# Rows of f2 by DMA through DRAM instead of transposes and a spreading matmul, in a two-layer graph attention kernel

## The chip, the core and the metric

The kernel runs on one core of a Trainium2 chip. The metric is the device time of one execution in microseconds: median 1540.99 of 3 runs (1539.92 to 1544.33). All times below are microseconds unless marked ns.

## The reference

For each of 16 graphs (512 nodes, 256 features), one shared adjacency:

```
h   = relu(layernorm(x))
for each of 4 heads:  Wh = h @ W[head]                       # 512 x 256
    f1 = Wh @ a1[head];  f2 = Wh @ a2[head]                  # one number per node
    e[n, m] = leaky_relu(f1[n] + f2[m], 0.01);  masked by adj # 512 x 512
    out[head] = elu(softmax(e) @ Wh)
then the same attention once more ("BACK") on the 4 joined heads (W_out, a_out)
y   = relu(out @ w1 + b1) @ w2 + b2 + out;  x = x + layernorm(y) * gamma + beta
h   = relu(layernorm(x))
x   = x + deg * (h @ Wi.T + b) + adj @ (h @ Wj.T)
```

What matters here is f2: it is made as a column (one number per node, nodes on the partitions) and is needed as a row in every partition, to be added to the mask and reduced to each row's maximum.

## The kernel before

All weights, the mask and the transposed adjacency stay in SBUF. The loop goes over the 16 batches (graphs), software-pipelined: every engine has an order table, `(step, info, late)`, written out by hand at the head of the file. In round t an engine goes through its table once and does each step for batch t - late (19 rounds in all, the first and last partly empty). Each engine executes in order; steps of different engines are tied by semaphores. TensorE computes the products in float32r with a high and a low part of each operand, thus three matmuls per product.

A batch has ten units: heads 0 and 1, BACK, heads 2 and 3, each in two halves of 256 rows (two groups of 128). A unit goes: `rowmax` (VectorE, L604 to L611: f2 row plus mask, written to `arg`, maximum to `gmax`), `rowmath`, `args` (ScalarE, two leaky relus and two exponentials in place), `turn_p` (TensorE, eight transposes to psR), `probs` (ScalarE the high part, VectorE the low part), `attend` (24 matmuls), `elu_in`, `elu_low` (GpSimd), `elu_exp`, `elu_out`. `arg` has ARGS = 3 buffers; a row max of unit u waits until `turn_p` of unit u - 3 is done.

The other steps of a round: `turn_in` and `m1` (eight of 12 matmuls, one per head and half; VectorE's part of it reads psA into `whx_lo` and `fcol`), `turn2` and `mix2` (four each: eight transposes of `hcat`, 24 matmuls), `turn_out`, `ffn1`, `ffn2`, `norm_ff`, `gamma` and `x_beta` (GpSimd), `x2`, `norm_gc`, `turn_gc`, `conv_in`, `conv`. Four double banks of PSUM: psA0, psA1 in turn for all wide products, psR for `turn_p`, psT (banks T0 and T1) for all else, among it the transposes of `turn2`.

f2 of heads before: `f2rows` (L590 to L602 on VectorE, L762 to L769 on TensorE, L406 to L409 on ScalarE) takes the columns of two heads from `fcol`, splits them into a high and a low part, turns them by four transposes into 4 rows of bank T0 and copies these to `f2row`. Then `spread` (L771 to L781) puts the sum of the two rows of a head into all 128 partitions of a bank of psT by one matmul with a 0/1 matrix `pick`; the bank stays taken until the head's second row max has been made. Three f2rows (heads 0 and 1, BACK, heads 2 and 3) and five spreads a round. SP's queue holds only a load, a store and a `load_back` of 512 KB for each batch; the load_back waits for the store's landing.

Of the kernel before, what the change touches and what calls it, by code (L numbers as in the profile page):

```python
# [921 lines left out]
```

## Time and profile before

| | |
|---|---|
| median of the runs | 1540.99 |
| the profiled execution's own time | 1542.53 |
| its span, first to last instruction | 1540.7 |
| TensorE busy | 1428.9 (93%) |
| VectorE, ScalarE, GpSimd busy | 1136.4, 1066.9, 236.3 |
| mean granted TensorE clock | 0.974 of full speed |
| moved by DMA | 33.04 MB |

Busy time of an engine is the time in which at least one of its instructions runs; matmuls are pipelined, so that several overlap, and the busy time of a group of matmuls can be more than what the group costs. An entry of the timeline gives start and length. Idle time stands in brackets with what ended it. PE is TensorE, DVE VectorE, ACT ScalarE, POOL GpSimd, SPq the DMA queue of SyncE.

### The profile page before, as it was taken

The numbers are of one execution on the slowest core, as the hardware profiler recorded it, in microseconds if no ns is written. First come the engines' busy times: TensorE is split into PE (matmuls) and PEld (weight loads), VectorE is DVE, ScalarE is ACT, GpSimd is POOL, SyncE is SP. The second block draws the span as 40 slices with busy tenths as digits, with TensorE's granted clock in tenths as the row PEclk, the third lists the DMA queues.
The fourth block names the chain that finished last, engine by engine and source line by source line (L and its number), as shares of the span: only waits on it lengthen the run. The fifth ranks groups of instructions, "written<-read, shape, count | busy, mean of one in ns | idle before, by whom it ended". The sixth has DMA issues, their size and how long they took to land.

```text
span 1540.7 us, 28639 instructions
## 1 busy us (share of the span) xinstructions
PE 1428.9 (93%) x10792; PEld 1333.2 (87%) x10792; DVE 1136.4 (74%) x2836; ACT 1066.9 (69%) x1700; POOL 236.3 (15%) x254
## 2 busy tenths in 40 slices
PE   1589999999999999999999999999999999999883
PEld 1479899999999999999999999999999999999762
DVE  6666778687778868687887868787886878787533
...
DMA packets 30056, 33.04 MB, mean 21 GB/s; under 512 B 1248, under 2 KB 28896, under 8 KB 29792
## 3 DMA queue, kind: packets, MB, share of 16 engines
q1 hardware_dynamic: 29920, 31.20, 6.3%
...
q14 instruction: 48, 0.39, 0.1%
...
## 4 chain that ended last, share of the span: by engine, by line
PE 81%; ACT 8%; DVE 7%; issue 3%; DMA 0%; POOL 0%; POOLq 0%; DVEq 0%; ACTq 0%
PE psA L736 52%; PE psR L789 8%; PE psT L890 4%; PE psT L814 4%; PE psA L848 4%; PE psA L859 4%; ACT ff L389 2%; ACT arg L420 1%; DVE hx_lo L577 1%; PE psT L780 1%; ACT prob_hi L426 1%; ACT hx_hi L441 1%; PE psT L768 1%; DVE arg L609 1%; PE psT L747 1%
## 5 line engine op out<-in xcount | busy, mean ns | idle before, releaser
L736 PE MATMUL psA<-whx_hi,prob_hi 128*128 128x258 f32 x1024 | 303.4, 296 | 14.2 <-DVE fcol L588 13.6
L736 PE MATMUL psA<-whx_hi,prob_lo 128*128 128x258 f32 x1024 | 291.0, 284 | 0.0
L736 PE MATMUL psA<-whx_lo,prob_hi 128*128 128x256 f32 x1024 | 289.9, 283 | 0.0
L577 DVE TENSOR_TENSOR prob_lo<-psR,prob_hi 128x1024 fp32r<-128x1024 f32 x160 | 195.2, 1220 | 55.5 <-ACT prob_hi L426 55.3
L356 POOL TENSOR_SCALAR elu_ex<-elu_in 128x512 f32<-128x512 f32 x160 | 103.4, 646 | 854.1 <-ACT elu_in L432 702.1
L609 DVE CUSTOM_DVE_ANT_0 arg<-psT,mask 128x512 f32<-128x512 f32 x320 | 208.0, 687 | 27.4 <-PE psT L780 24.4
L416 ACT ACTIVATE arg<-arg,fcol 128x512 f32<-128x512 f32 x320 | 212.5, 714 | 18.0 <-DVE gmax L609 18.0
L420 ACT ACTIVATE arg<-arg,nmax 128x512 f32<-128x512 f32 x320 | 212.0, 712 | 10.5 <-DVE nmax L620 10.5
L736 PEld LDWEIGHTS psA<-whx_hi,prob_hi 128*128 128x128 f32 x1024 | 195.8, 191 | 23.0 <-issue 17.8
L736 PEld LDWEIGHTS psA<-whx_hi,prob_lo 128*128 128x128 f32 x1024 | 194.9, 190 | 4.9 <-issue 3.6
L736 PEld LDWEIGHTS psA<-whx_lo,prob_hi 128*128 128x128 f32 x1024 | 195.6, 191 | 0.0
L426 ACT ACTIVATE prob_hi<-psR 128x1024 fp32r<-128x1024 f32 x160 | 163.1, 1019 | 45.2 <-PE psR L789 44.5
L789 PE MATMUL psR<-ident,arg 128*128 128x128 f32 x1280 | 168.2, 275 | 17.3 <-ACT arg L420 9.0
L789 PEld LDWEIGHTS psR<-ident,arg 128*128 128x128 f32 x1280 | 144.9, 142 | 25.3 <-ACT arg L420 13.9
L736 PE MATMUL psA<-wh_hi,hT_hi 128*128 128x258 f32 x512 | 153.5, 300 | 6.4 <-DVE fcol L588 4.0
L736 PE MATMUL psA<-wo_hi,hx_hi 128*128 128x258 f32 x512 | 147.9, 289 | 0.0
L736 PE MATMUL psA<-wh_lo,hT_hi 128*128 128x258 f32 x512 | 146.0, 285 | 0.0
L736 PE MATMUL psA<-wh_hi,hT_lo 128*128 128x258 f32 x512 | 145.7, 285 | 0.0
L736 PE MATMUL psA<-wo_hi,hx_lo 128*128 128x258 f32 x512 | 145.0, 283 | 0.0
L736 PE MATMUL psA<-wo_lo,hx_hi 128*128 128x258 f32 x512 | 144.9, 283 | 0.0
L404 ACT ACTIVATE whx_hi<-psA 128x512 fp32r<-128x512 f32 x128 | 76.4, 597 | 88.3 <-PE psA L736 88.3
L642 DVE SCALAR_TENSOR_TENSOR hcat<-elu_ex,elu_in 128x512 f32<-128x512 f32 x128 | 111.3, 869 | 27.2 <-ACT elu_ex L436 27.2
...
## 6 DMA issues: line engine op xcount, KB each, us to landing
xin<-in_x SPq DMA_DIRECT2D x16, 512.0 KB, 4.0
xb<-in_x SPq DMA_DIRECT2D x16, 512.0 KB, 3.9
out_x<-xb SPq DMA_DIRECT2D x16, 512.0 KB, 2.9
...
hcat<-in_L_gnn_W_heads SPq DMA_DIRECT2D x2, 512.0 KB, 8.1
...
xb<-in_L_gnn_W SPq DMA_DIRECT2D x1, 512.0 KB, 6.6
```

What stands on the lines that cost most here:

```text
L356: pool.tensor_scalar(elu_ex[:, c.buf, :, :], elu_in[:, c.buf, :, :], 0.0, -3.0e38, ALU.min, ALU.max).then_inc(elu_low, 1)
L404: act.activation(whx[:, 2 * p:2 * p + 2, h, 0:F], psA[c.pair][:, :, 0:F], ACT.Copy).then_inc(m1_hi, 1)
L416: act.activation(a[:, n, :], a[:, n, :], ACT.Prelu, bias=f1[:, n:n + 1], alpha=SLOPE).then_inc(arg_lin, 1)
L420: i = act.activation(a[:, n, :], a[:, n, :], ACT.Exp, bias=nmax[:, c.abuf, n:n + 1])
L426: act.activation(prob[0][:, c.buf, :, :].rearrange("p j i -> p (j i)"), psR[:, :, :].rearrange("p a n -> p (a n)"), ACT.Copy).then_inc(pro ...
L577: return dve.tensor_tensor(out=dst, in0=src, in1=hi.bitcast(fp32), op=ALU.subtract)
L609: dve.tensor_tensor_reduce(out=arg[:, c.abuf, n, :], in0=psT[:, bank_of(c.h), :], in1=mask[:, 2 * c.u + n, :], scale=1.0, scalar=-3.0e38, ...
L642: dve.scalar_tensor_tensor(out=dst, in0=elu_ex[:, c.buf, :, :], scalar=-1.0, in1=elu_in[:, c.buf, :, :], op0=ALU.add, op1=ALU.max).then_in ...
L736: i = pe.matmul(o, a, b_, start=(k == 0), stop=(k == n - 1))
L789: i = pe.transpose(p[:, j, n, :], arg[:, c.abuf, n, j * P:(j + 1) * P], ident[:, :])
L814: i = pe.transpose(psT[:, k // 4, (k % 4) * P:(k % 4 + 1) * P], hcat[:, n, k // KC, (k % KC) * P:(k % KC + 1) * P], ident[:, :])
L848: i = pe.matmul(psA[c.pair][:, o, :], w1_sb[:, k, o * P:(o + 1) * P], outT[:, k, :], start=(k == 0), stop=(k == KC - 1))
```

## The change

`f2rows` and `spread` go from all three tables. In their place SP has a step `f2` for each head: it waits for the column in `fcol` (or `fcol2`), issues a DMA of the 512 numbers to one of four rows of a DRAM scratch, waits for its landing, and issues a DMA that reads this row into all 128 partitions of one of F2S = 3 buffers `f2bc` in SBUF. The row max waits for that landing and reads `f2bc` in place of psT. ARGS goes from 3 to 2, and a row max waits for `turn_p` of unit u - 2. `c1`, `f2row`, their memsets and semaphores go; a spill buffer of the setup moves from `arg` to `f2bc`. All five order tables are written anew. The diff shows the tables of SP and TensorE before and after, and those of the other engines after.

```diff
-    ("load", 0, 3), ("store", 0, 6), ("load_back", 0, 5),
+    ("store", 0, 4), ("load_back", 0, 3), ("load", 0, 0), ("f2", 0, 1), ("f2", 1, 1), ("f2", -1, 2), ("f2", 2, 1),
+    ("f2", 3, 1),
...
 PE_STEPS = [
-    ("conv", 0, 3), ("turn_p", 7, 1), ("attend", 6, 1), ("turn_out", 0, 2), ("turn_p", 8, 1), ("attend", 7, 1),
-    ("ffn1", 0, 2), ("attend", 8, 1), ("turn_p", 9, 1), ("ffn2", 0, 2), ("turn2", 0, 1), ("attend", 9, 1), ("turn2", 1, 1),
-    ("mix2", 0, 1), ("turn_in", 0, 0), ("mix2", 1, 1), ("turn2", 2, 1), ("m1", (0, 0), 0), ("m1", (0, 1), 0),
-    ("turn2", 3, 1), ("m1", (1, 0), 0), ("m1", (1, 1), 0), ("m1", (2, 0), 0), ("f2rows", 0, 0), ("m1", (2, 1), 0),
-    ("spread", (0, 0), 0), ("mix2", 2, 1), ("mix2", 3, 1), ("spread", (0, 1), 0), ("turn_p", 0, 0), ("m1", (3, 0), 0),
-    ("m1", (3, 1), 0), ("turn_p", 1, 0), ("turn_gc", 0, 2), ("attend", 0, 0), ("f2rows", 2, 1), ("turn_p", 2, 0),
-    ("spread", (2, 0), 1), ("attend", 1, 0), ("conv_in", 0, 2), ("f2rows", 1, 0), ("turn_p", 3, 0), ("attend", 2, 0),
-    ("turn_p", 4, 1), ("spread", (1, 0), 0), ("conv_in", 1, 2), ("attend", 3, 0), ("turn_p", 5, 1), ("spread", (1, 1), 0),
-    ("attend", 4, 1), ("turn_p", 6, 0), ("attend", 5, 1),
+    ("mix2", 0, 2), ("turn2", 2, 2), ("mix2", 1, 2), ("m1", (2, 0), 1), ("turn2", 3, 2), ("turn_p", 0, 1), ("m1", (2, 1), 1),
+    ("mix2", 2, 2), ("mix2", 3, 2), ("turn_p", 1, 1), ("attend", 0, 1), ("turn_p", 2, 1), ("turn_gc", 0, 3),
+    ("attend", 1, 1), ("m1", (3, 0), 1), ("turn_p", 3, 1), ("m1", (3, 1), 1), ("conv_in", 0, 3), ("attend", 2, 1),
+    ("turn_p", 4, 2), ("conv_in", 1, 3), ("attend", 3, 1), ("turn_p", 5, 2), ("attend", 4, 2), ("turn_p", 6, 1),
+    ("conv", 0, 3), ("attend", 5, 2), ("turn_p", 7, 1), ("attend", 6, 1), ("turn_p", 8, 1), ("attend", 7, 1),
+    ("turn_out", 0, 2), ("attend", 8, 1), ("turn_p", 9, 1), ("ffn1", 0, 2), ("turn_in", 0, 0), ("attend", 9, 1),
+    ("m1", (0, 0), 0), ("turn2", 0, 1), ("ffn2", 0, 2), ("m1", (0, 1), 0), ("m1", (1, 0), 0), ("turn2", 1, 1),
+    ("m1", (1, 1), 0),
...
 ACT_STEPS = [
...
+    ("m1", (0, 0), 1), ("turn2", 0, 2), ("m1", (0, 1), 1), ("elu_exp", 9, 2), ("m1", (1, 0), 1), ("turn2", 1, 2),
+    ("m1", (1, 1), 1), ("norm_ff_out", 0, 3), ("turn2", 2, 2), ("args", 0, 1), ("mix2", 0, 2), ("m1", (2, 0), 1),
+    ("turn2", 3, 2), ("args", 1, 1), ("probs", 0, 1), ("m1", (2, 1), 1), ("args", 2, 1), ("mix2", 1, 2), ("probs", 1, 1),
+    ("norm_gc_out", 0, 3), ("probs", 2, 1), ("elu_in", 0, 1), ("turn_gc", 0, 3), ("args", 3, 1), ("elu_in", 1, 1),
+    ("m1", (3, 0), 1), ("elu_exp", 0, 1), ("probs", 3, 1), ("elu_exp", 1, 1), ("m1", (3, 1), 1), ("args", 4, 2),
+    ("conv_in", 0, 3), ("args", 5, 2), ("elu_in", 2, 1), ("probs", 4, 2), ("conv_in", 1, 3), ("elu_exp", 2, 1),
+    ("args", 6, 1), ("probs", 5, 2), ("elu_in", 3, 1), ("elu_exp", 3, 1), ("elu_in", 4, 2), ("probs", 6, 1),
+    ("elu_exp", 4, 2), ("args", 7, 1), ("args", 8, 1), ("probs", 7, 1), ("elu_in", 5, 2), ("norm_in_out", 0, 0),
+    ("elu_exp", 5, 2), ("probs", 8, 1), ("elu_in", 6, 1), ("args", 9, 1), ("turn_out", 0, 2), ("elu_in", 7, 1),
+    ("elu_exp", 6, 1), ("elu_exp", 7, 1), ("probs", 9, 1), ("elu_in", 8, 1), ("elu_exp", 8, 1), ("turn_in", 0, 0),
+    ("ffn1", 0, 2), ("elu_in", 9, 1),
 ]
 DVE_STEPS = [
...
+    ("ffn2", 0, 3), ("norm_ff", 0, 3), ("m1", (0, 1), 1), ("m1", (1, 0), 1), ("turn2", 1, 2), ("m1", (1, 1), 1),
+    ("norm_ff_out", 0, 3), ("elu_out", 9, 2), ("rowmax", 0, 1), ("rowmath", 0, 1), ("rowmax", 1, 1), ("turn2", 2, 2),
+    ("x2", 0, 3), ("mix2", 0, 2), ("rowmath", 1, 1), ("m1", (2, 0), 1), ("turn2", 3, 2), ("rowmax", 2, 1), ("rowmath", 2, 1),
+    ("norm_gc", 0, 3), ("probs", 0, 1), ("m1", (2, 1), 1), ("norm_gc_out", 0, 3), ("mix2", 1, 2), ("probs", 1, 1),
+    ("rowmax", 3, 1), ("elu_in", 0, 1), ("rowmath", 3, 1), ("probs", 2, 1), ("turn_gc", 0, 3), ("elu_in", 1, 1),
+    ("rowmax", 4, 2), ("rowmath", 4, 2), ("m1", (3, 0), 1), ("rowmax", 5, 2), ("rowmath", 5, 2), ("elu_out", 0, 1),
+    ("m1", (3, 1), 1), ("probs", 3, 1), ("conv_in", 0, 3), ("elu_in", 2, 1), ("rowmax", 6, 1), ("rowmath", 6, 1),
+    ("elu_out", 1, 1), ("probs", 4, 2), ("conv_in", 1, 3), ("elu_out", 2, 1), ("elu_in", 3, 1), ("rowmax", 7, 1),
+    ("probs", 5, 2), ("elu_in", 4, 2), ("rowmath", 7, 1), ("norm_in", 0, 0), ("rowmax", 8, 1), ("norm_in_out", 0, 0),
+    ("rowmath", 8, 1), ("probs", 6, 1), ("elu_out", 3, 1), ("elu_out", 4, 2), ("conv", 0, 3), ("elu_in", 5, 2),
+    ("probs", 7, 1), ("elu_in", 6, 1), ("rowmax", 9, 1), ("rowmath", 9, 1), ("elu_out", 5, 2), ("probs", 8, 1),
+    ("elu_in", 7, 1), ("elu_out", 6, 1), ("elu_in", 8, 1), ("probs", 9, 1), ("elu_out", 7, 1), ("turn_in", 0, 0),
+    ("elu_out", 8, 1), ("elu_in", 9, 1), ("m1", (0, 0), 0), ("turn2", 0, 1),
 ]
 POOL_STEPS = [
...
+    ("gamma", 0, 3), ("norm_gc", 0, 3), ("elu_low", 0, 1), ("elu_low", 1, 1), ("elu_low", 2, 1), ("elu_low", 3, 1),
+    ("elu_low", 4, 2), ("norm_in", 0, 0), ("elu_low", 5, 2), ("elu_low", 6, 1), ("x_beta", 0, 2), ("elu_low", 7, 1),
+    ("elu_low", 8, 1), ("elu_low", 9, 1), ("norm_ff", 0, 2),
...
-    ARGS = 3
+    ARGS = 2
+    F2S = 3
...
-        c1 = [sb(f"c1_{q}", [P, NC, 2, 2]) for q in range(3)]
...
-        f2row = sb("f2row", [P, N], f32r)
+        f2bc = sb("f2bc", [P, F2S, N])
+        f2_rows = nc.dram_tensor("f2_rows", (4, N), fp32, kind="Internal").ap()
...
+            def f2(c):
+
+                h = c.info
+                head = unit_number[c.b, h, 0] // 2
+                if h == BACK:
+                    sp.wait_ge(m2_read, 2 * (c.b + 1))
+                    column = fcol2[:, :, 0, 1]
+                else:
+                    sp.wait_ge(m1_read, 2 * H * c.b + 2 * h + 2)
+                    column = fcol[:, :, h, 1]
+                wait(sp, max_made, 4 * (head - F2S + 1))
+                sp.dma_start(f2_rows[head % 4].rearrange("(n q) -> q n", q=P), column, allow_slow_non_contiguous=True).then_inc(f2_out, 16)
+                sp.wait_ge(f2_out, 16 * (head + 1))
+                sp.dma_start(f2bc[:, head % F2S, :], f2_rows[head % 4].partition_broadcast(P)).then_inc(f2_spread[head % F2S], 16)
+
...
-            def f2rows(c):
-                q = c.info
-                act.wait_ge(c1_turned[q], c.b + 1)
-                act.activation(f2row[0:4, :], psT[0:4, 0, :], ACT.Copy).then_inc(f2row_made[q], 1)
-
...
             def rowmax(c):
 
-                dve.wait_ge(f2_spread, c.unit // 2 + 1)
+                head = c.unit // 2
+                dve.wait_ge(f2_spread[head % F2S], 16 * (head // F2S + 1))
                 wait(dve, p_turned, c.unit - ARGS + 1)
                 for n in range(2):
-                    dve.tensor_tensor_reduce(out=arg[:, c.abuf, n, :], in0=psT[:, bank_of(c.h), :], in1=mask[:, 2 * c.u + n, :],
+                    dve.tensor_tensor_reduce(out=arg[:, c.abuf, n, :], in0=f2bc[:, head % F2S, :], in1=mask[:, 2 * c.u + n, :],
                                              scale=1.0, scalar=-3.0e38, op0=ALU.add, op1=ALU.max,
                                              accum_out=gmax[:, c.abuf, n:n + 1]).then_inc(max_made, 1)
 
...
-            def f2rows(c):
-                q = c.info
-                pe.wait_ge(c1_made[q], 2 * (c.b + 1))
-                take("T0")
-                for n in range(NC):
-                    i = pe.transpose(psT[0:4, 0, n * P:(n + 1) * P], c1[q][:, n, :, :].rearrange("p a h -> p (a h)"), ident[:, :])
-                i.then_inc(c1_turned[q], 1)
-                lend(("T0",), (f2row_made[q], c.b + 1))
-
-            def spread_(c):
-
-                q, hh = c.info
-                h0, _ = heads_of(q)
-                h = h0 if h0 == BACK else h0 + hh
-                pe.wait_ge(f2row_made[q], c.b + 1)
-                bank = f"T{bank_of(h)}"
-                take(bank)
-                pe.matmul(psT[:, bank_of(h), :], pick[:, hh, :], f2row[:, :], start=True, stop=True).then_inc(f2_spread, 1)
-                lend((bank,), (max_made, 2 * unit_number[c.b, h, 1] + 2))
-
```

## Rows read from the trace of the kernel before

**Rows 1.** The page: busy us, share of the span and instructions of each engine.

```profile
PE 1428.9 (93%) x10792; PEld 1333.2 (87%) x10792; DVE 1136.4 (74%) x2836; ACT 1066.9 (69%) x1700; POOL 236.3 (15%) x254
```

**Rows 2.** The windows: busy us (and instructions) of each engine in one steady round.

```profile
700.00:788.04 88.04, 87.28 (x674) 81.83 (x672) 68.54 (x171) 65.75 (x107) 14.64 (x15) 1.00 0.06 19
```

**Rows 3.** The waits of PE between 200 and 1400 us: total, times, longest.

```profile
PE psR L789 <- ACT arg L420: 3.9, 14, 0.3
```

**Rows 4.** Groups by line, all of the span: busy us, mean ns; idle before, releaser.

```profile
L780 PE MATMUL psT<-f2row,pick 128*128 128x512 f32 x80 | 35.6, 447 | 0.8 <-ACT f2row L409 0.8
...
L768 PE MATMUL psT<-ident,c 128*4 128x128 f32 x192 | 29.1, 275 | 3.5 <-DVE h2T_lo L577 2.5 <-DVE gmax L609 0.8 <-DVE c L602 0.2
```

**Rows 5.** The timeline of PE at a spreading matmul and at four transposes: start, length.

```profile
752.89 0.39 PE L780 MATMUL psT<-f2row,pick 128*128 128x512 f32 x1
753.12 0.28 PE L736 MATMUL psA<-wo_hi,hx_hi 128*128 128x258 f32 x1
...
776.07 0.60 PE L768 MATMUL psT<-ident,c 128*4 128x128 f32 x4
776.50 0.27 PE L789 MATMUL psR<-ident,arg 128*128 128x128 f32 x1
```

**Rows 6.** Groups by line of VectorE and ScalarE on the new chain.

```profile
L416 ACT ACTIVATE arg<-arg,fcol 128x512 f32<-128x512 f32 x320 | 212.5, 714 | 18.0 <-DVE gmax L609 18.0
...
L609 DVE CUSTOM_DVE_ANT_0 arg<-psT,mask 128x512 f32<-128x512 f32 x320 | 208.0, 687 | 27.4 <-PE psT L780 24.4 <-PE psR L789 2.9
...
L577 DVE TENSOR_TENSOR hx_lo<-psT,hx_hi 128x1024 fp32r<-128x1024 f32 x64 | 78.4, 1225 | 16.8 <-ACT hx_hi L441 15.9
...
L558 DVE BATCH_NORM_STATS2 st<-wk 128x6 f32<-128x256 f32 x64 | 22.4, 413 | 0.0
...
L660 DVE TENSOR_TENSOR wk<-psA,wk 128x1024 f32<-128x1024 f32 x16 | 19.3, 1209 | 12.5 <-PE psA L859 12.5
...
L563 DVE BATCH_NORM_AGGREGATE mv_ff<-st 128x2 f32<-128x6 f32 x64 | 6.1, 157 | 1.7
...
L515 DVE CUSTOM_DVE_ANT_0 arg<-hcat,ff 128x256 f32<-128x256 f32 x16 | 5.8, 419 | 0.1
```

**Rows 7.** The timeline of VectorE and GpSimd at 727 us, and gamma's group by line.

```profile
727.59 2.19 DVE L642 SCALAR_TENSOR_TENSOR hcat<-elu_ex,elu_in 128x512 f32<-128x512 f32 x1 [0.68 <-ACT elu_ex L436]
...
726.87 2.36 POOL L360 TENSOR_TENSOR xb<-xb,beta_bc 128x1024 f32<-128x1024 f32 x1
...
L365 POOL TENSOR_TENSOR wk<-wk,gamma_bc 128x1024 f32<-128x1024 f32 x16 | 38.2, 2390 | 71.3 <-ACT wk L389 71.3
```

**Rows 8.** The timeline of SP's queue: the store and the load_back that waits for it.

```profile
447.19 0.38 SPq L324 DMA_DIRECT2D out_x<-xb  x1
450.18 0.37 SPq L320 DMA_DIRECT2D xb<-in_x  x1
```

**Rows 9.** DMA: the queue's share; issues with KB and us to landing; b1c's issue.

```profile
q1 hardware_dynamic: 29920, 31.20, 6.3%
...
xb<-in_x SPq DMA_DIRECT2D x16, 512.0 KB, 3.9
...
gamma_bc<-in_L_gnn_ln_gamma SPq DMA_DIRECT2D x1, 128.0 KB, 6.3
...
b1c<-in_L_gnn_b SPq DMA_DIRECT2D x1, 1.0 KB, 7.7
...
11.55 0.88 SPq L308 DMA_DIRECT2D b1c<-in_L_gnn_b  x1
```

**Rows 10.** The timeline of PE: first and last matmul of an attend, the transposes behind.

```profile
700.03 0.28 PE L736 MATMUL psA<-w2x_hi,prob_lo 128*128 128x258 f32 x1
...
702.77 1.04 PE L789 MATMUL psR<-ident,arg 128*128 128x128 f32 x8
703.56 0.36 PE L736 MATMUL psA<-w2x_hi,prob_hi 128*128 128x258 f32 x1
```

**Rows 11.** The timeline of PE in the drain, with its wait in brackets.

```profile
1465.44 1.01 PE L768 MATMUL psT<-ident,c 128*4 128x128 f32 x4 [2.47 <-DVE h2T_lo L577]
```

More of the change, by code:

```diff
@@ L37 @@
-    ("m1", (2, 1), 1), ("rowmax", 2, 1), ("norm_gc_out", 0, 3), ("mix2", 1, 2), ("probs", 0, 1), ("rowmax", 3, 1),
-    ("m1", (3, 0), 1), ("f2rows", 2, 2), ("rowmath", 2, 1), ("probs", 1, 1), ("turn_gc", 0, 3), ("elu_in", 0, 1),
-    ("m1", (3, 1), 1), ("rowmath", 3, 1), ("f2rows", 1, 1), ("rowmax", 4, 2), ("rowmath", 4, 2), ("rowmax", 5, 2),
-    ("probs", 2, 1), ("elu_in", 1, 1), ("rowmath", 5, 2), ("conv_in", 0, 3), ("probs", 3, 1), ("elu_out", 0, 1),
-    ("elu_in", 2, 1), ("rowmax", 6, 1), ("rowmath", 6, 1), ("rowmax", 7, 1), ("probs", 4, 2), ("conv_in", 1, 3),
@@ L42 @@
-    ("elu_out", 1, 1), ("rowmath", 7, 1), ("elu_in", 3, 1), ("rowmax", 8, 1), ("probs", 5, 2), ("elu_out", 2, 1),
-    ("elu_in", 4, 2), ("rowmax", 9, 1), ("rowmath", 8, 1), ("rowmath", 9, 1), ("probs", 6, 1), ("elu_out", 3, 1),
-    ("elu_in", 5, 2), ("norm_in", 0, 0), ("elu_out", 4, 2), ("elu_out", 5, 2), ("conv", 0, 3), ("probs", 7, 1),
-    ("elu_in", 6, 1), ("probs", 8, 1), ("elu_in", 7, 1), ("elu_out", 6, 1), ("elu_in", 8, 1), ("elu_out", 7, 1),
-    ("norm_in_out", 0, 0), ("elu_out", 8, 1), ("probs", 9, 1), ("ffn2", 0, 2), ("turn2", 0, 1), ("norm_ff", 0, 2),
@@ L47 @@
-    ("elu_in", 9, 1), ("turn2", 1, 1), ("norm_ff_out", 0, 2), ("elu_out", 9, 1), ("turn_in", 0, 0), ("mix2", 0, 1),
-    ("turn2", 2, 1), ("m1", (0, 0), 0),
+    ("ffn2", 0, 3), ("norm_ff", 0, 3), ("m1", (0, 1), 1), ("m1", (1, 0), 1), ("turn2", 1, 2), ("m1", (1, 1), 1),
+    ("norm_ff_out", 0, 3), ("elu_out", 9, 2), ("rowmax", 0, 1), ("rowmath", 0, 1), ("rowmax", 1, 1), ("turn2", 2, 2),
+    ("x2", 0, 3), ("mix2", 0, 2), ("rowmath", 1, 1), ("m1", (2, 0), 1), ("turn2", 3, 2), ("rowmax", 2, 1), ("rowmath", 2, 1),
@@ L49 @@
 ]
 POOL_STEPS = [
-    ("norm_gc", 0, 3), ("elu_low", 0, 1), ("elu_low", 1, 1), ("elu_low", 2, 1), ("elu_low", 3, 1), ("elu_low", 4, 2),
-    ("elu_low", 5, 2), ("elu_low", 6, 1), ("elu_low", 7, 1), ("norm_in", 0, 0), ("elu_low", 8, 1), ("x_beta", 0, 2),
-    ("norm_ff", 0, 2), ("elu_low", 9, 1), ("gamma", 0, 2),
+    ("gamma", 0, 3), ("norm_gc", 0, 3), ("elu_low", 0, 1), ("elu_low", 1, 1), ("elu_low", 2, 1), ("elu_low", 3, 1),
+    ("elu_low", 4, 2), ("norm_in", 0, 0), ("elu_low", 5, 2), ("elu_low", 6, 1), ("x_beta", 0, 2), ("elu_low", 7, 1),
@@ L176, in gnn_kernel @@
         m1_read = sem("m1_read")
-        c1_made = [sem(f"c1_made{q}") for q in range(3)]
-        c1_turned = [sem(f"c1_turned{q}") for q in range(3)]
-        f2row_made = [sem(f"f2row_made{q}") for q in range(3)]
-        f2_spread = sem("f2_spread")
+        f2_out = sem("f2_out")
+        f2_spread = [sem(f"f2_spread{i}") for i in range(F2S)]
         m2_turned = sem("m2_turned")
@@ L324, in store @@
                 sp.dma_start(out_v[c.b], xb[:, :, :]).then_inc(stored, 16)
-            run_all(SP_STEPS, {"load": load, "load_back": load_back, "store": store})
+            run_all(SP_STEPS, {"load": load, "f2": f2, "load_back": load_back, "store": store})
             sp.wait_ge(stored, 16 * B)
@@ L340, in _ @@
                 pool.wait_ge(s_const, 2 + z)
-            pool.memset(f2row[:, :].bitcast(fp32), 0.0)
-            for q in range(3):
-                i = pool.memset(c1[q][:, :, :, :], 0.0)
-            i.then_inc(s_cleared, 1)
             def norm(k):
@@ L689, in _ @@
             run_all(DVE_STEPS, {"norm_in": norm("in", xin, x_loaded, 16), "norm_in_out": norm_out("in"), "turn_in": turn_in, "m1": m1,
-                                "f2rows": f2rows, "rowmax": rowmax, "rowmath": rowmath, "probs": probs, "elu_in": elu_in_,
+                                "rowmax": rowmax, "rowmath": rowmath, "probs": probs, "elu_in": elu_in_,
                                 "elu_out": elu_out_, "turn2": turn2, "mix2": mix2, "ffn2": ffn2,
@@ L893, in conv @@
                 lend(T, (res_ready, c.b + 1))
-            run_all(PE_STEPS, {"turn_in": turn_in, "m1": m1, "f2rows": f2rows, "spread": spread_, "turn_p": turn_p,
+            run_all(PE_STEPS, {"turn_in": turn_in, "m1": m1, "turn_p": turn_p,
                                "attend": attend, "turn2": turn2, "mix2": mix2, "turn_out": turn_out, "ffn1": ffn1, "ffn2": ffn2,
```

33 lines of the change are left out of this document (2 added, 31 removed), and 3 rows, old and new, of the table ACT_STEPS.

## The prediction

> **What bounds the kernel now.** I read the page's busy shares first: TensorE is busy for 93% of the span, VectorE 74% [rows 1]. Then the windows. One steady batch (a round of the order tables) takes 88.04 us from one batch's spreading matmul to the next one's; in it TensorE is busy 87.28, VectorE 68.54, ScalarE 65.75, GpSimd 14.64 us, at granted clock 1.00, the upper level of 2.4 GHz [rows 2]. That leaves 0.76 us a round in which TensorE isn't busy. Third, its waits between 200 and 1400 us: the longest group is 3.9 us in 14 times, none over 0.3 [rows 3]. So in the steady part the time is the sum of TensorE's instructions; a microsecond taken off it is won only if nothing else becomes late, and VectorE, the next engine, has 20 us of room per round on average, but it works strictly in its written order.
>
> **The change part by part.**
>
> *Removed from TensorE.* Per round three groups of four transposes (48 groups, x192) and five spreading matmuls (x80); as busy time 29.1 + 35.6 = 64.7 us in all, 3.6 to 4.0 per round [rows 4]. Busy times of pipelined matmuls overlap, so I price by distances of starts. A spread starts at 752.89 and the next matmul at 753.12: 0.23 us, five of them 1.15. A group of four transposes holds 0.43 (776.07 to 776.50): three of them 1.3 [rows 5]. A matmul behind transposes is longer by 0.08 (0.36 at 703.56 against 0.28 at 700.03 [rows 10]), and four such changes go: 0.3. Sum 2.8 us a round, 16 rounds: **45 us off**. Bounds: 2.5 (40 us) and the busy time, 58 us (3.6 a round).
>
> *Removed elsewhere.* ScalarE loses 48 copies of the f2 rows and VectorE 96 small operations on the columns: neither engine is the sum, so this counts nothing by itself; it is cover for the rest. The memsets at the start lie beside loads: nothing.
>
> *Row max from SBUF instead of PSUM.* The same operation with both operands in SBUF stands in the setup: 128x256 in 420 ns, against 687 ns for 128x512 from PSUM [rows 6]. The slope between them is (687 - 420) / 256 = 1.04 ns an element, that of VectorE's other rows from either memory: no gain, no loss, taken as 0 (bounds -0.1 and +0.1 us an instruction). But now it reads two SBUF operands, and the trace has a row of what that can mean: an elu_out, whose operands are both in SBUF, took 2.19 us from 727.59 (a row max of that size 0.69), and ended 0.55 us after GpSimd's 2.36 us addition that had begun at 726.87 [rows 7]. It stood still until GpSimd was through, and the new row max can do the same. The Trainium skill, page "SBUF — State Buffer", says why: a VectorE instruction with two SBUF inputs and a GpSimd instruction that reads SBUF need the same shared port, held for a whole instruction, and the later one waits. By that rule the old row max (one operand in PSUM) was exempt and the new one is not, and a row max that meets gamma loses all of it, which gives rival 2's 1541; the row on elu_out agrees with the rule, while the row alone leaves open how often they meet.
>
> *The new chain of f2.* Per head SP issues a DMA of 512 single elements from the column to a DRAM row, waits until it has landed, and issues the broadcast of that row to 128 partitions. The trace has neither. Nearest rows: SP begins the store at 447.19, and the load_back that waits for its landing begins at 450.18, 2.99 us on [rows 8]; a load lands in 3.9 [rows 9]. Of that the 512 KB themselves are 1.6 us: 31.2 MB took 6.3% of 1540.7 us, 0.32 MB/us [rows 9]. So a nearly empty store is 3.0 - 1.6 = 1.4, plus the longer issue of single elements (0.88 in the queue against 0.38, b1c against the store [rows 8, 9]) 0.5, plus 0.3 that I grant 512 elements: 2.2. The broadcast is 256 KB: 3.9 - 1.6 + 0.8 = 3.1. Sum **5.3 us**. High ends from the crowded start: b1c's 256 single elements landed in 7.7, gamma's broadcast in 6.3 [rows 9], together 14; these queued behind megabytes, so I stay at the quiet rows. Low end 4.5. The Trainium skill, page "DMA: Bandwidth & Descriptors" (Specifications), says that under 512 B a DMA reads, modifies and writes; no row prices that for a write to DRAM, and it would push the first term up only.
>
> *Where that chain lies.* Four of the five heads have much time; head 0 does not. In the new order TensorE has, between the end of ffn2 and turn2(3), 96 matmuls at 0.119 (23 starts from 700.03 to 702.77) = 11.4 and two groups of eight transposes at 0.87 (0.79 and the change): **13.2 us** [rows 10]. What must be done in that time stands in VectorE's order, one after the other: ffn2's addition 1.21, norm_ff's four statistics 4 x 0.35 = 1.4 and aggregations (0.16 each, in series with the addition behind) 0.7, m1(0,1)'s reading 0.76 (half of turn2's subtraction and a copy), then the f2 chain 5.3, then the row max of units 0 and 1 (four at 208.0 / 320 = 0.65, and rowmath between) 2.9, then turn2(2)'s subtraction 1.2, which frees the psT banks for turn2(3): **13.5 us** [rows 6]. So TensorE is 0.3 us late there in each round, and every microsecond more in the DMA chain is one more. turn2(2), x2, mix2(0) and m1(2,0) of VectorE stand behind the waiting row max, and turn_p(0), mix2(2) and m1(2,1) of TensorE wait for them. I add the port: gamma on GpSimd (2.39 us [rows 7]) waits for norm_ff's output on ScalarE, which follows VectorE's norm_ff_out just before elu_out(9) and rowmax(0): by the durations it becomes ready within 0.3 us of the f2 row. Either it gets between the four row maxima and VectorE loses up to 2.4 us, or it waits for them and x2 is late by some 1.1. I take 1.0, less than either, since the instants are uncertain. **Together 1.3 us lost a round, 21 us.** Bounds: 0 (both hidden), and 8.9 a round with the 14 us chain.
>
> *ARGS from 3 to 2.* A row max now waits for the transposes of two units before. From row max to finished exponentials is 1.3 + 2.7 us by the pace of the ScalarE row (four at 212.5 / 320 = 0.66) [rows 6]; between turn_p(k) and turn_p(k+2) the new TensorE order has at least two attends and a turn_p and some other step, 9 us. Hidden by 5 us; without that cover it would cost a microsecond a unit.
>
> *Queues.* SP's five f2 steps hold it some 5 x 3 us a round. The store and load_back stand behind f2 of head 3, which is issued about 15 us before conv ends: not held. x_beta then needs store 3.0 + load_back 3.9 after conv's addition, two attends later: hidden by about 1 us. POOL gets x_beta before elu_low(7) as before. PSUM banks T0 and T1 no longer hold f2 for 2 units; VectorE's 24.4 us of waits for the spreading matmul go [rows 6], on an engine that is not the sum: 0.
>
> *Fill and drain.* From turn_in to the end of conv is 237 us in both orders by counting steps. In the fill head 0 no longer waits for head 1, which pays for the DMA; in the drain TensorE already idles 2.47 us before the last f2rows [rows 11], and gc work covers most. I take +2 (0 to +10).
>
> Sum: own time of the profiled execution 1542.53; 1542.5 - 45 + 21 + 2 = 1520.5. The median of the runs is 1.5 below that execution: **1519 us**.
>
> **The rivals.**
> 1. *The DMA chain is the new bound.* From 7.8 us on it eats all: 45 - 2 = 43 us over 16 rounds is 2.7 lost a round, 0.3 plus 2.4 beyond 5.3. At 9 us with the port: 1541 (the execution's 1542.5 less 1.5) - 45 + 2 + 16 x (0.3 + 3.7 + 1.0) = 1578; without it 1562. For it: 512 single elements, for which only the 7.7 us row stands, and head 0's place without slack. Against: a full 512 KB store comes back in 3.0. Chance 0.17.
> 2. *The port takes the rest.* gamma between the row maxima each round, 2.4 + 0.3: 1541 - 45 + 2 + 43 = 1541, no change. For it the 2.19 us row; against, GpSimd is busy for 17% of a round only [rows 2]. Chance 0.13.
> 3. *All of it is won.* Chain under 5 us, GpSimd misses VectorE: 1541 - 45 + 2 = 1498, by busy time 1485. For it, the old order's 0.3 us waits [rows 3] show how well such an order can fit together. Chance 0.2.
> 4. That it doesn't do what it says can't be: the steps are gone from TensorE's table.
>
> **How the numbers follow.** My forecast (lost 0.7 to 2.2 a round, 1509 to 1533) has 0.5. The range reaches to rivals 3 and 1 in part: 1492 to 1555. A measurement here tells about 0.3%, 4.6 us. Faster: forecast 0.5, rival 3's 0.2, and a bit of rival 2: 0.72; same 0.09; slower 0.19.
>
> **What would show it.** Right: TensorE 2.8 to 3.6 us less busy a round, no psT matmul of 512 columns; a round of about 86.5 us; VectorE's wait for the broadcast at rowmax(0) of each round 1 to 2 us; TensorE waits of 1 to 2 us a round at turn2(3), m1(2,1) or turn_p(0); single row maxima of 1 to 3 us beside GpSimd's gamma. Wrong: an f2 DMA pair above 7 us, waits at all heads, or a round of 85.3 or under.

## The result, and the profile after

The kernel after takes 1794.07 us (median of 4 runs, 1788.28 to 1797.6) against 1540.76 before (4 runs): ratio 1.1635, 95% interval 1.1599 to 1.1672. It is 16% slower, where 1519 us had been forecast with 1492 to 1555 as range. The page of the kernel after: busy shares as in [rows 1], the group that answers to L609 of [rows 6], the queue as in [rows 9], the chain that ended last, and the two f2 transfers (KB each, us to landing; the page gives none for the write).

```profile
PE 1455.3 (81%) x10520; PEld 1371.2 (77%) x10520; DVE 1100.6 (62%) x2740; ACT 1048.6 (59%) x1652; POOL 239.1 (13%) x250
...
q1 hardware_dynamic: 83680, 52.35, 15.6%
...
PE 49%; DMA 31%; DVE 14%; issue 3%; ACT 1%; POOL 0%; SPq 0%; POOLq 0%; DVEq 0%; ACTq 0%
...
L589 DVE CUSTOM_DVE_ANT_0 arg<-f2bc,mask 128x512 f32<-128x512 f32 x320 | 212.8, 702 | 306.6 <-DMA f2bc<-f_rows 299.5
...
f2bc<-f_rows SPq DMA_DIRECT2D x80, 256.0 KB, 4.8
...
f_rows<-fcol SPq DMA_DIRECT2D x80, 2.0 KB
```

The row max itself costs what it did (702 ns, 687 before), but VectorE stands 299.5 us before it for the broadcast, and 31% of the chain is DMA. The timeline of SP in a steady round has both transfers (L318 writes the column, L320 waits for it and broadcasts):

```profile
752.21 0.37 SPq L318 DMA_DIRECT2D f_rows<-fcol  x1
760.26 0.34 SPq L320 DMA_DIRECT2D f2bc<-f_rows  x1
760.70 0.38 SPq L318 DMA_DIRECT2D f_rows<-fcol  x1
771.35 0.33 SPq L320 DMA_DIRECT2D f2bc<-f_rows  x1
782.68 0.36 SPq L318 DMA_DIRECT2D f_rows<-fcol  x1
790.49 0.33 SPq L320 DMA_DIRECT2D f2bc<-f_rows  x1
790.92 0.38 SPq L318 DMA_DIRECT2D f_rows<-fcol  x1
801.89 0.33 SPq L320 DMA_DIRECT2D f2bc<-f_rows  x1
```

The writes are those of head 0 (752.21), head 1, BACK (782.68) and head 2. L318 to L320 is the column write with its landing: 8.05 us where 2.2 were forecast, 7.81 for BACK, 10.65 and 10.97 when it begins behind a broadcast. The broadcast of head 0 then lands at 765.05, 4.8 us on. VectorE's first row max and what stands behind it, then TensorE at the transposes that it holds up, turn2(3):

```profile
765.05 0.69 DVE L589 CUSTOM_DVE_ANT_0 arg<-f2bc,mask 128x512 f32<-128x512 f32 x1 [8.97 <-DMA f2bc<-f_rows]
...
767.94 1.22 DVE L570 TENSOR_TENSOR hx_lo<-psT,hx_hi 128x1024 fp32r<-128x1024 f32 x1
```
```profile
769.31 1.94 PE L774 MATMUL psT<-ident,hcat 128*128 128x128 f32 x8 [7.22 <-DVE hx_lo L570]
```

The second wait of the round is BACK's. VectorE's copy of BACK's column, its first row max of BACK, and TensorE at conv_in, which needs a PSUM buffer that VectorE reads only behind that row max:

```profile
782.51 0.15 DVE L636 COPY fcol<-psA 128x4 f32<-128x4 f32 x1
...
795.43 0.69 DVE L589 CUSTOM_DVE_ANT_0 arg<-f2bc,mask 128x512 f32<-128x512 f32 x1 [4.92 <-DMA f2bc<-f_rows]
```
```profile
797.95 0.77 PE L716 MATMUL psA<-wg_hi,h2T_hi 128*128 128x512 f32 x1 [4.45 <-DVE fcol L581]
```

BACK's write starts at 782.68, as soon as its column is there: it doesn't queue behind another head's. Heads 1, 2 and 3 do queue behind another transfer, and neither of the two long waits is theirs. The windows of the round, and of the two stretches right behind the waits (column order as in [rows 2]):

```profile
752.21:765.00 12.79, 9.77 (x80) 9.58 (x80) 3.29 (x7) 4.64 (x7) 2.81 (x2) 1.00 0.11 21
765.00:775.00 10.00, 5.69 (x27) 5.72 (x28) 7.96 (x19) 7.23 (x12) 0.00 (x0) 0.50 0.24 16
775.00:795.00 20.00, 18.50 (x155) 18.12 (x154) 12.46 (x34) 15.46 (x25) 2.24 (x3) 1.00 0.08 20
795.00:805.00 10.00, 7.05 (x30) 6.09 (x31) 7.31 (x21) 4.24 (x7) 0.00 (x0) 0.66 0.21 7
805.00:853.85 48.85, 48.73 (x368) 45.38 (x366) 35.79 (x87) 33.50 (x55) 9.76 (x11) 1.00 0.19 43
sum 101.64, PE 89.74 PEld 84.89 DVE 66.81 ACT 65.08 POOL 14.80; mean PE 17.95 PEld 16.98 DVE 13.36 ACT 13.02 POOL 2.96
```
```profile
769.30:775.00 5.70, 5.69 (x27) 5.70 (x28) 3.79 (x8) 4.33 (x8) 0.00 (x0) 0.50 0.42 28
797.95:802.00 4.05, 4.05 (x11) 3.29 (x12) 3.80 (x10) 1.39 (x3) 0.00 (x0) 0.50 0.00 0
```

A round takes 101.64 us. Before it took 88.43, not the 88.04 of [rows 2]: one batch's spreading matmul starts at 699.60 and the next one's at 788.03, and that window began at 700.00.

```profile
699.60:788.03 88.43, 87.67 (x677) 82.18 (x675) 68.91 (x171) 66.14 (x108) 14.64 (x15) 1.00 0.06 19
```

TensorE idles 11.9 us of the round after, and after each of the two long waits the granted clock is low: 0.50 (the 1.2 GHz level) for 5.70 us behind the 7.22 us wait, and 0.50 for 4.05 us behind the 4.45 us one. The work of these stretches runs at half pace: that is why busy PE rose.

Where the 8 us of the write go can't be read from the queue's share. The DMA view of the same write, all queues, first from 752.4 to 753.6, then from 753.6 to the moment SP goes on:

```profile
DMA  0000000000000000000000016799878886300000
...
DMA packets 528, 0.00 MB, mean 2 GB/s; under 512 B 528, under 2 KB 528, under 8 KB 528
```
```profile
DMA packets 0, 0.00 MB, mean 0 GB/s; under 512 B 0, under 2 KB 0, under 8 KB 0
```

All 528 packets are over by 753.5; then 6.8 us pass without a packet until the write counts as landed. The Trainium skill, "DMA: Bandwidth & Descriptors", section on the anatomy of one DMA (written of DMAs that GpSimd issues), says that most of a DMA's fixed 2 us is the receipt for the write in the target memory, longest for DRAM. The place agrees with this trace, the size doesn't: 6.8 us.

### The profile page after: what moved, and what is told of

It is laid out like the page before. It is cut to its first block, busy times and chain, and to the rows that moved or that the text cites. A ratio compares the mean times of both kernels' runs of the same rounds, so it can differ in the third digit from the quotient of the medians.

```text
span 1786.5 us, 28037 instructions
## 1 busy us (share of the span) xinstructions
PE 1455.3 (81%) x10520; PEld 1371.2 (77%) x10520; DVE 1100.6 (62%) x2740; ACT 1048.6 (59%) x1652; POOL 239.1 (13%) x250
## 4 chain that ended last, share of the span: by engine, by line
PE 49%; DMA 31%; DVE 14%; issue 3%; ACT 1%; POOL 0%; SPq 0%; POOLq 0%; DVEq 0%; ACTq 0%
PE psA L716 30%; DMA f_rows<-fcol 21%; DMA f2bc<-f_rows 10%; PE psR L749 5%; PE psT L850 3%; PE psA L808 3%; PE psA L819 3%; DVE arg L589 3%; DVE st L551 2%; PE psT L774 2%; DVE whx_lo L570 1%; DVE prob_lo L570 1%; DVE wk L640 1%; PE psT L796 1%; PE psT L727 1%
## 5 line engine op out<-in xcount | busy, mean ns | idle before, releaser
L589 DVE CUSTOM_DVE_ANT_0 arg<-f2bc,mask 128x512 f32<-128x512 f32 x320 | 212.8, 702 | 306.6 <-DMA f2bc<-f_rows 299.5
L749 PE MATMUL psR<-ident,arg 128*128 128x128 f32 x1280 | 185.5, 293 | 56.8 <-DVE prob_lo L570 35.8
L749 PEld LDWEIGHTS psR<-ident,arg 128*128 128x128 f32 x1280 | 159.9, 153 | 62.1 <-issue 39.1
L774 PE MATMUL psT<-ident,hcat 128*128 128x128 f32 x512 | 79.9, 308 | 121.4 <-DVE hx_lo L570 119.8
L716 PE MATMUL psA<-wh_hi,hT_hi 128*128 128x258 f32 x512 | 158.5, 309 | 6.1 <-DVE fcol L581 3.7
L774 PEld LDWEIGHTS psT<-ident,hcat 128*128 128x128 f32 x512 | 67.7, 160 | 124.4 <-issue 122.5
L716 PE MATMUL psA<-wh_hi,hT_lo 128*128 128x258 f32 x512 | 149.3, 292 | 0.0
```

What stands on the lines that cost most here:

```text
L589: dve.tensor_tensor_reduce(out=arg[:, c.abuf, n, :], in0=f2bc[:, head % F2S, :], in1=mask[:, 2 * c.u + n, :], scale=1.0, scalar=-3.0e38, o ...
L716: i = pe.matmul(o, a, b_, start=(k == 0), stop=(k == n - 1))
L749: i = pe.transpose(p[:, j, n, :], arg[:, c.abuf, n, j * P:(j + 1) * P], ident[:, :])
L774: i = pe.transpose(psT[:, k // 4, (k % 4) * P:(k % 4 + 1) * P], hcat[:, n, k // KC, (k % KC) * P:(k % KC + 1) * P], ident[:, :])
```

## The experiments

**What the column write costs: without it, and without both transfers.** The first leaves out every column write after the fourth head (the broadcast reads an old row, so f2 is another head's); the second leaves out both DMAs after the third head.

```diff
+                if head < 4:
                     sp.dma_start(f2_rows[head % 4]...).then_inc(f2_out, 16)
                     sp.wait_ge(f2_out, 16 * (head + 1))
```
```diff
+                if head >= F2S: return
...
-                dve.wait_ge(f2_spread[head % F2S], 16 * (head // F2S + 1))
+                dve.wait_ge(f2_spread[head % F2S], 16)
```

> The column is written to DRAM only for the first four heads; after that SP goes straight to the broadcast of an old row (f2 of the right head is left out). Theory A (the write of 512 single elements is the cost, 8.05 us issue to landing in the changed kernel's trace): the chain of head 0 falls from 12.9 to 4.8 us, below the 5.3 of the prediction, so 1500 to 1520 us. Theory B (the new order, two arg buffers or the SBUF operands are slow by themselves): stays above 1600 us. Theory C (the broadcast of one DRAM row, 4.8 us, and SP's waiting in order carry half): 1600 to 1680.

> Both DMAs of f2 are left out after the first three heads; row maxima read old rows and wait for nothing of them. What is left is the new order with f2 for free. Theory A: 1498 us (1541 - 45 + 2), rival 3 of the prediction, TensorE waits under 1 us a round, clock at its upper level throughout. Theory B: above 1600. If it is 1515 to 1530, the port and gamma cost the 1 us a round that the prediction set for them.

Measured: 1513.14 us, ratio 0.9815 (0.9795 to 0.9835), and 1508.01, ratio 0.9782 (0.9766 to 0.9799). The steady round of the first (the second's is 85.24):

```profile
723.27:808.50 85.23, 84.64 (x658) 80.54 (x658) 68.97 (x165) 64.75 (x103) 15.63 (x15) 1.00 0.12 35
```

85.23 against 88.43 before: the removed transposes and spreads are worth 3.2 us a round, forecast 2.8. Against 101.64 the column write costs 16.4 a round: 11.9 - 0.6 = 11.3 as idle TensorE, 89.74 - 84.64 = 5.1 as work at the lower clock. Times 16 that is 262 of the 281 us between the two times. The broadcast alone costs 5 us in the whole run (1513 against 1508). With no transfer left the kernel is still 10 above the 1498 of my third rival: in its first 180 us TensorE is busy 104.7 us, before 117.3, and its waits there add up to 75.0 for 62.7, so this is the fill.

The second run also shows the port. Timelines of VectorE and GpSimd:

```profile
822.12 0.69 DVE L591 CUSTOM_DVE_ANT_0 arg<-f2bc,mask 128x512 f32<-128x512 f32 x1
822.74 2.90 DVE L591 CUSTOM_DVE_ANT_0 arg<-f2bc,mask 128x512 f32<-128x512 f32 x1
```
```profile
822.14 2.95 POOL L367 TENSOR_TENSOR wk<-wk,gamma_bc 128x1024 f32<-128x1024 f32 x1 [5.11 <-ACT wk L391]
```

A row max beside gamma takes 2.90 in place of 0.69, as the forecast feared, yet the round is 85.24, with 0.6 us of TensorE idle: where the row max has no transfer to wait for, the loss of 2.2 is hidden.

**Is it the size of the pieces?** The columns are laid out so that a partition's four numbers lie together; the write then has 128 pieces of 16 bytes, in the order (q n), and the row max reads row, mask and arg at the step that undoes it. It computes the reference's result.

```diff
-                sp.dma_start(f2_rows[head % 4].rearrange("(n q) -> q n", q=P), column, ...)
+                sp.dma_start(f2_rows[head % 4].rearrange("(q n) -> q n", q=P), column)
...
-                                             in0=f2bc[:, head % F2S, :], ...
+                                             in0=f2bc[:, head % F2S, :].rearrange("p (q n) -> p n q", q=P), ...
```

> f2 of a head lies contiguous in each partition (16 bytes), is written by 128 pieces of 16 bytes instead of 512 of 4, and the row max reads the row with a step of four elements. Theory A1 (each separate write to DRAM costs about the same, (8.05 - 1.8) / 512 x 16 engines = 0.2 us): the write falls to 1.8 + 1.6 = 3.4 us, the chain to 8.2, loss per round 0.3 + 2.9, time about 1550 to 1580. Theory A2 (a small write to DRAM has a fixed long receipt): still 8 us, 1780 to 1800. Theory A3 (the strided read by VectorE is slower): row max above 0.8 us, visible in its mean.

Measured 1627.96, ratio 1.0556 (1.0531 to 1.0581). The write lands in 1.4 alone, where 3.4 were expected, in 2.6 and 2.8 at heads 0 and 1 and in 5.4 behind a broadcast. Most of what is left is the row max: reading every fourth element from SBUF takes 1090 ns (median) for 687, 1185 in the mean; with the same write and a row max without the step the kernel takes 1545 (below).

**Single writes, by themselves.** One DMA at a time, SP from issue to issue; computes nothing of the reference. Each series of single writes ran once, with every kind four times.

> Single DMAs, each waited for before the next is issued; nothing else of the kernel is computed. Theory A1 (time per separate write): 512 elements 8.0 us, 256 elements 4.9, 128 elements 3.4, 128 pieces of 16 bytes 3.4, 4 pieces of 512 bytes under 2.2; elements with 512 bytes between them also 8.0. Theory A2 (fixed receipt): all small writes 8. Theory A4 (many writes into the same 512 bytes of DRAM are what is slow): the 512 elements spaced by 512 bytes under 4 us. Broadcast of one row of 2 KB to 128 partitions 4.8 us if one row is read by all engines slowly, against 3.1 for 128 own rows of 2 KB.

```profile
3.20 0.39 SPq L41 DMA_DIRECT2D full<-strided  x1
14.01 0.36 SPq L41 DMA_DIRECT2D half<-strided  x1
23.08 0.33 SPq L41 DMA_DIRECT2D quarter<-strided  x1
31.29 0.36 SPq L41 DMA_DIRECT2D sparse<-strided  x1
33.74 0.33 SPq L41 DMA_DIRECT2D by<-packed  x1
35.16 0.32 SPq L41 DMA_DIRECT2D by<-four  x1
36.35 0.34 SPq L41 DMA_DIRECT2D bc<-by  x1
39.39 0.37 SPq L41 DMA_DIRECT2D own<-in_x  x1
```

The next row's start less the row's own: 512 neighbours of four bytes 10.8 us, 256 of them 9.1, 128 still 8.2; the same 512 elements each 512 bytes from the next 2.45; 128 pieces of 16 bytes 1.42; four of 512 bytes 1.19; the broadcast 3.04. The number of pieces doesn't make the write slow (128 of four bytes 8.21, 128 of 16 bytes 1.42), nor does it that they are small (spaced, they take 2.45), nor that they are neighbours (pieces of 16 bytes are too): it takes both, pieces of four bytes that are neighbours in DRAM. (Over four repeats: 9.3 to 11.3, 8.8 to 10.2, 7.4 to 8.2, 2.45 to 3.0.) The Trainium skill, "DMA: Bandwidth & Descriptors" (Specifications), has a read, modify and write for everything under 512 bytes; by this trace that alone isn't what costs here, since the spaced elements are as small.

> Single DMAs, each waited for. 512 elements of 4 bytes with 4, 8, 16, 32, 64 and 128 bytes from one to the next in DRAM; then 256 pieces of 8 bytes, 128 of 16, a broadcast; last a broadcast with the write of 512 neighbouring elements right behind it. Theory A4 (pieces of different engines in one stretch of DRAM disturb each other; with 512 bytes between them the write took 2.7): 9 us at 4 bytes, falling to 2.7 where each piece, or each run of four that one engine writes, has its own stretch: at 16 bytes if that stretch is 64 bytes, at 128 if it is 512. Theory A1 (cost per piece) is out already, since 128 elements took 8.2. Write behind a broadcast: 11 us or more, as in the kernel.

A finer row: 512 elements at a step of 4 bytes 8.0 to 9.6 us, 8 bytes 2.9 to 3.1, 16 bytes 2.5 to 2.6, 32 to 128 bytes 1.8 to 2.1. 256 neighbouring pieces of eight bytes took 3.1 to 4.1.

**The same in the kernel: only the addresses changed.** The write keeps elements, waits and order, but goes to a scratch with 512 bytes to an element; the broadcast reads an old row, so f2 is another head's.

```diff
+                row = f2_rows[head % 4] if head < 4 else f2_spaced[head % 4, :, 0]
-                sp.dma_start(f2_rows[head % 4].rearrange("(n q) -> q n", q=P), column, ...)
+                sp.dma_start(row.rearrange("(n q) -> q n", q=P), column, ...)
```

> The changed kernel, but from the fifth head on the 512 elements go to a scratch in which each has 512 bytes of its own, and the broadcast reads an old row (f2 of the right head is left out). Same number and size of elements, same waits, same order. Theory A4 (neighbours in DRAM are the cost): the chain is 2.7 + 3.3 = 6.0 us, 0.7 above the prediction's, so 1515 to 1535 us. If the kernel's surroundings make the write slow whatever the addresses: above 1700.

Measured 1528.04, ratio 0.9911 (0.9898 to 0.9924); the write takes 1.8 to 2.3 (4.3 behind a broadcast). The DMA view of one write from its issue at 775.99 to its landing at 777.76, in 40 slices, has its 528 packets over by 777.2: it lands 0.5 us on, where 528 packets to neighbours took 6.8.

```profile
DMA  0000000000000000000037987884000000000000
```

So 266 us of the 1794 are the address pattern, and with a write at the forecast's price the kernel lies within 9 us of the forecast. Its round, the first two row maxima of head 0, and gamma beside them:

```profile
727.36:813.96 86.60, 84.65 (x658) 80.56 (x658) 68.92 (x165) 64.74 (x103) 15.34 (x15) 1.00 0.12 35
```
```profile
745.66 0.69 DVE L591 CUSTOM_DVE_ANT_0 arg<-f2bc,mask 128x512 f32<-128x512 f32 x1 [1.26 <-DMA f2bc<-f_rows]
...
746.28 2.88 DVE L591 CUSTOM_DVE_ANT_0 arg<-f2bc,mask 128x512 f32<-128x512 f32 x1
```
```profile
745.99 2.62 POOL L367 TENSOR_TENSOR wk<-wk,gamma_bc 128x1024 f32<-128x1024 f32 x1 [5.07 <-ACT wk L391]
```

The chain is 5.16 us (740.50 to 745.66), forecast 5.3. Gamma gets between the row maxima, as in the second run above, and VectorE's wait of 1.26 us comes on top; the round is 1.4 us longer than without the write (86.60 against 85.23), where 1.3 were forecast for chain and port together.

**The order of the work.** Slow write kept; m1(0, 1), the last part of head 0's column, goes ahead of turn2(0), ffn2 and norm_ff in the tables of TensorE, ScalarE and VectorE.

```diff
-    ("m1", (0, 0), 0), ("turn2", 0, 1), ("ffn2", 0, 2), ("m1", (0, 1), 0), ("m1", (1, 0), 0), ("turn2", 1, 1),
+    ("m1", (0, 0), 0), ("m1", (0, 1), 0), ("turn2", 0, 1), ("ffn2", 0, 2), ("m1", (1, 0), 0), ("turn2", 1, 1),
```

> The changed kernel with its slow DMAs, only m1(0,1) is put ahead of turn2(0) and ffn2 on TensorE, and ahead of turn2(0), ffn2 and norm_ff on VectorE, so that the column of head 0 is ready some 6 us earlier. Theory A (TensorE is late by the chain less the work above it, in a fixed place): the wait at turn2(3), 7.2 us a round, falls to about 1 to 2; head 1's chain and BACK's stay. 16 rounds by 5 to 6 us and up to 2 us of clock each: 1670 to 1710. Rival (SP's queue is the bound, the five chains one after the other, 5 x 13 us = 65 us and two further transfers in 101): less than 20 us gained.

Measured 1708.37, ratio 1.108 (1.1064 to 1.1096). TensorE's waits at L774 fall from 119.8 to 45.0 us; those for the copy at BACK stay (82.5 for 83.5). So head 0's lack of slack had cost at least these 86 us, three tenths of the 281; BACK's wait and 45 us at L774 are left. The rival, SP's queue as the bound, had allowed less than 20 us.

**Who should pay for the order of the nodes.** Three kernels with 16-byte pieces, all computing the reference's result. In the first the mask is permuted once in the setup, and turn_p takes every fourth column of `arg`; in the second the row max writes `arg` with a step and turn_p is as before; the third is the first with the early m1(0, 1).

```diff
-                i = pe.transpose(p[:, j, n, :], arg[:, c.abuf, n, j * P:(j + 1) * P], ident[:, :])
+                i = pe.transpose(p[:, j, n, :], arg[:, c.abuf, n, :].rearrange("p (q j) -> p j q", q=P)[:, j, :], ident[:, :])
```
```diff
-                    dve.tensor_tensor_reduce(out=arg[:, c.abuf, n, :], ...
+                    dve.tensor_tensor_reduce(out=arg[:, c.abuf, n, :].rearrange("p (j q) -> p q j", q=P), ...
```

> The changed kernel, but f2 is written as 128 pieces of 16 bytes, so that the row in DRAM stands in the order (partition, chunk); the mask is laid down once in that order, row max reads and writes without a step, and turn_p takes every fourth column of arg as its input. Theory A (the write of 4-byte neighbours is the whole loss): the chain of head 0 is 1.4 + 3.3 to 4.1 = 4.7 to 5.5 us as single DMAs measured, about the 5.3 of the prediction; 1513 to 1525 us, faster than both kernels. Rival (the transposes read arg with a step of 16 bytes and get slower, eight a unit, 80 a round): over 1530, with transposes longer than 0.27 us in the trace. The 1628 us of the version with the strided row max would be wholly VectorE's 1.19 us a row max.

> Pieces of 16 bytes as in the run where the transposes read every fourth column, but here the row max undoes the order itself: it reads row and mask in the order in which they lie and writes arg with a step, so that exp, the transposes and everything behind them are those of the change. Theory A (in that run it was the transposes, 142 to 210 ns each in the weight load, that gave back what the faster column brought): the column write stays at 1.4 to 2.8 us, the weight loads of L752 are back at 142 ns, and the time is that of the run with spaced elements or better, 1515 to 1530 us; the row max may take 0.7 to 1.1 us for each, on an engine that has the time. Rival B (it was the order of the work, with the chain of the column still late): 1540 to 1550 us whatever the transposes cost. Rival C (a stepped write in SBUF costs the row max as much as the stepped read did, some 1.1 us, and where it is last it delays TensorE): 1530 to 1560 us with TensorE waiting for the transposes' operand.

> 16-byte pieces with transposes that read every fourth column, and in addition m1(0, 1) of a round, which gives the last half of the right head's column, stands before turn2(0), ffn2 and the norm on all three engines, as in the run of that order with the slow write. Theory A (what is left of the cost of that run is in the transposes' weight loads, not in waits; its waits for hx_lo were only 29 us over the whole run): 1535 to 1545 us, at most 8 us below the 1545 without the move. Rival B (waits for the column still decide): 1520 to 1530 us.

Measured: 1545.16, ratio 1.0016 (1.0004 to 1.0028); 1612.2, ratio 1.046 (1.0444 to 1.0475); **1510.5, ratio 0.98 (0.9784 to 0.9817)**. The stepped row max with the early m1(0, 1) was 1571.26 (1.0195), 41 below the stepped one alone, where I had expected the two within 5 us. Of the second kernel the row max and the transposes' loads, then the same of the third:

```profile
L592 DVE CUSTOM_DVE_ANT_0 arg<-f2bc,mask 128x512 f32<-128x512 f32 x320 | 364.9, 1218 | 33.5 <-DMA f2bc<-f_rows 27.1
...
L754 PEld LDWEIGHTS psR<-ident,arg 128*128 128x128 f32 x1280 | 156.2, 150 | 49.9 <-issue 39.8
```
```profile
L592 DVE CUSTOM_DVE_ANT_0 arg<-f2bc,mask 128x512 f32<-128x512 f32 x320 | 242.4, 794 | 15.3 <-PE psR L752 13.1
...
L752 PEld LDWEIGHTS psR<-ident,arg 128*128 128x128 f32 x1280 | 169.2, 209 | 33.3 <-issue 22.8
```

I had blamed the transposes and was wrong: they lose 0.09 a group of eight (0.88 from 744.98 to 745.86, 0.79 in [rows 10]), 0.9 a round. The step on VectorE costs 0.42 us (1218 less 794 ns) in each of 20 row maxima a round, on an engine that works in strict order with TensorE behind it. And my theory for the third was wrong by 25 us: the waits for hx_lo, 29.2 us in the first, are 5.9 in the third, but the moved step won 35 us. The 12 that the waits leave over are busy time of TensorE, 1394.1 us for 1406.5 with the same 10520 instructions: in the first kernel a round with clock 0.98 is busy for 87.04, one with 1.00 for 85.48. The round of the third:

```profile
712.46:798.55 86.09, 85.30 (x658) 81.46 (x658) 68.52 (x165) 64.85 (x103) 15.60 (x15) 1.00 0.14 35
```

86.09 is 85.23 plus those 0.9: in the steady round all of the removal is won but for the transposes. It beats the kernel before by 31 us (2.0%), and the kernel after by 284.

**What in neighbours is slow.** Two more series of single writes, 128 elements of four bytes.

> Single writes of a column of 128 elements of four bytes to DRAM, one after the other, each kind four times, times from issue to issue; it computes nothing of the reference. Neighbours (7.4 to 8.2 us before) against: one element and a gap of one; two and a gap of two; four and a gap of four (each stretch of 32 bytes then holds only one run of four partitions); eight and a gap of eight; and neighbours from 8 or from 4 partitions only. Theory A (the slow thing is a stretch of 32 bytes that is written by more than one DMA engine, each run of four partitions being one engine's): four and a gap of four is fast, 1.5 to 2.5 us, eight and a gap of eight is slow again, 6 to 8, and 4 partitions alone are fast, 8 partitions slow in part, 3 us or more. Rival B (any element that shares its stretch of bytes with a neighbour costs, whoever writes it): four and a gap of four stays at 6 to 8 us, and only the elements with gaps of one win in part. Rival C (it is the number of elements): nothing but the 8 and the 4 partitions gets faster.

> Single writes again, each kind four times, times from issue to issue; it computes nothing of the reference. 128 elements of four bytes as neighbours (6.6 to 8.9 us before), with a gap of eight after every eight (3.1), with a gap of 16 after every 16, 32 after 32, 64 after 64, and neighbours from 16, 32 and 64 partitions alone. So far: four bytes at steps of 4, 8, 16 and 32 bytes took 8 to 9, 3.0, 2.6 and 1.9 us, whatever their count. Theory A (elements that fall into the same stretch of 64 bytes are taken one after the other by the memory: 16 to a stretch with neighbours, 8 and 4 and 2 with the steps): 16 after a gap of 16 is as slow as neighbours, 6 to 8 us, 32 and 64 too, and 16 partitions alone are already 5 us or more. Rival B (any gap makes the piece of DRAM that is written something else than one run, and the run of 512 bytes is what is slow): all four with gaps take about 3 us, and the time of neighbours grows with the partitions, from 1.1 us at 8. Rival C (a stretch longer than 64 bytes decides, so that the price grows step by step): 3 us at a gap of eight, 4 to 5 at 16, 6 at 32, 7 or more at 64, and the same series for 16, 32 and 64 partitions.

Neighbours 6.6 to 9.7 us; one element and a gap of one 2.7 to 3.3; two and two 3.1 to 3.7; four and four 3.0 to 3.7; eight and eight 3.1 to 3.7; 16 and 16 3.1 to 3.6; 32 and 32 3.9 to 4.4; 64 and a gap of 64 9.3 to 9.5. Neighbours from 4 or 8 partitions alone 1.1 to 1.2, from 16 1.3, from 32 4.8 to 5.2, from 64 6.9 to 7.4. The rules with a fixed stretch of 32 or 64 bytes fell, and so did "any gap helps"; how many elements lie in 512 bytes doesn't decide either, since every series with equal gaps has 64 of them and takes from 2.7 to 9.5. Nearest is that the price climbs with the length of the run of neighbours, steeply from 32 elements on, though four runs of 32 (3.9 to 4.4) took less than one alone. What the memory does in that time stays open.

## Why the prediction was wrong

- *What bounds it, and the removal:* the bound was right. The removal was priced too low: 3.2 us a round (88.43 against 85.23) for 2.8, and the window of 88.04 that I took for a round was 0.4 short.
- *Row max from SBUF:* right as to itself (702 ns for 687) and as to the port (2.90 beside gamma). In the kernel after, gamma runs while VectorE still waits for the broadcast (757.68 to 760.08), so nothing is lost to it: the longest row max takes 1.11. With the spaced write it falls between head 0's row maxima, as forecast, and chain and port together cost 1.4 a round for 1.3.
- *The new chain of f2:* here it failed. The column write, "plus 0.3 that I grant 512 elements: 2.2", measured 8.05 at head 0, and with it the chain was not 5.3 but 12.84 (752.21 to 765.05). I derived a write of single elements from a row of a store in whole rows, and read the queue's share as its price. The only row of single elements, b1c's 7.7 [rows 9], I set aside as crowded; 14 us as an upper end was nearer than 5.3, and the range should have held more of it. The broadcast, forecast 3.1, took 3.04 to 3.1 among the single writes, 3.3 in the kernel without the column write and 4.8 in the kernel after.
- *Where it lies:* place right, pace right. By "every microsecond more in the DMA chain is one more" 12.84 gives 0.3 + 7.5 = 7.8 late at turn2(3); measured 7.22.
- *"Four of the five heads have much time":* wrong with such a write. VectorE waited for 53 of 80 broadcasts, and BACK, whose slack was never worked out, costs TensorE 4.45 a round, though its write starts as soon as its column is there. SP, which "5 x 3 us a round" were to hold, stands 46.1 us a round for the five writes.
- *Not priced at all:* 5.1 us a round of TensorE at a lower granted clock after long waits. Rival 1 had the mechanism at 0.17 and stopped at 1578, since it took 9 us, one place and no clock. With the measured chain its own sum, 1498 + 16 x 7.8, gives 1623; the rest of the 1794 is mainly BACK's wait (16 x 4.45 = 71) and the clock (16 x 5.1 = 82).
- *Fill and drain:* +2, measured about +17 (1508 without transfers, against 1541 - 16 x 3.2 = 1490).
- *The 1528 with the spaced write* is nearer to 1519 than the terms were: the removal was worth 6 us more than forecast, the fill cost 15 more, and the two partly cancel.
